# First products of two experts: over 336 and then 112 columns, or once over all 448, with idle products in the wait

## What is computed

```
x = x + tanh(g_xattn) * attention(layernorm(x), ctx, w_q, w_k, w_v, w_o)
h = layernorm(x)
expert e (16 of them, 2 shared and 14 routed):
    silu((h * rsqrt(mean(h*h) + eps) * rms_w[e]) @ W1[e]) @ W2[e]      # 128 -> 256 -> 128
gates = softmax(h @ router_w), the two largest kept and scaled to sum 1
x = x + tanh(g_ffn) * (sum of shared experts + gated sum of routed experts)
```

## Time and profile before

| what | us |
|---|---|
| median of 3 runs | 121.24 |
| lowest and highest run | 121.11 and 122.18 |
| the profiled execution's own time | 121.09 |
| its span, first to last instruction | 119.3 |
| PE busy in it | 109.5 |
| DVE busy | 69.1 |
| ACT busy | 59.3 |
| POOL busy | 43.8 |

### The profile page before, as it was taken

The page is one execution under the profiler, slowest core; times in us unless marked ns, Lnnn a source line. Parts: engine busy times, 40 slices in busy tenths (PEclk is TensorE's granted clock), DMA queues, the critical chain, the costliest instruction groups (busy, mean ns, idle before and its releaser), DMA issues.

```text
span 119.3 us, 2340 instructions
## 1 busy us (share of the span) xinstructions
PE 109.5 (92%) x800; PEld 93.7 (79%) x800; DVE 69.1 (58%) x195; ACT 59.3 (50%) x99; POOL 43.8 (37%) x75
## 2 busy tenths in 40 slices
PE   6976999994999999999789989999999999999980
PEld 6965978763458559459569989999999999999980
DVE  0069857775749859959921626998633333333361
ACT  4072983439379578678674279423333323333300
POOL 7703599000000100100100578666666666664000
PEclk9999999997699999999999999999999999999999
DMA  3999999999991000000000000000000000000002
GB/s 104 334 273 370 413 419 408 417 434 438 426 410 63 3 0 0 0 0 5 0 0 5 0 0 5 3 0 3 0 0 5 0 0 0 0 0 0 0 0 77
DMA packets 3169, 13.76 MB, mean 115 GB/s; under 512 B 431, under 2 KB 1007, under 8 KB 2775
## 3 DMA queue, kind: packets, MB, share of 16 engines
q1 hardware_dynamic: 3159, 13.63, 29.9%
HBM read 13.40 MB, written 0.23 MB: 114 GB/s over the span
## 4 chain that ended last, share of the span: by engine, by line
PE 71%; DVE 17%; DMA 5%; ACT 3%; issue 1%; SPq 1%; DVEq 0%
PE score_ps L703 15%; PE attn_ps L703 7%; PE score_ps L514 7%; PE ring L696 6%; PE ring L697 5%; PE ring L698 5%; PE ring L557 5%; DMA ctx_headT<-in_ctx_headT_dram 5%; DVE probs L1007 4%; DVE row_sum L1000 3%; PE attn_ps L576 3%; PE ring L488 3%; PE ring L598 3%; PE ring L490 2%; PE ring L489 2%; PE score_ps L509 2%
## 5 line engine op out<-in xcount | busy, mean ns | idle before, releaser
L898 ACT ACTIVATE mixT<-ring 128x896 f32<-128x896 f32 x16 | 14.6, 917 | 27.0 <-PE ring L698 26.9
L703 PE MATMUL score_ps<-w,mixT 128*112 (+1 forms) x160 | 19.2, 273 | 0.2 <-ACT mixT L898 0.2
L703 PEld LDWEIGHTS score_ps<-w,mixT 128*112 128x112 f32 x160 | 18.7, 177 | 0.7 <-issue 0.3
L427 POOL TENSOR_TENSOR h_scale<-h_base,minus_half 112x1 f32<-112x1 f32 x4 | 2.2, 546 | 44.2 <-DVE h_base L1030 44.2
L1174 DVE SCALAR_TENSOR_TENSOR xn_rows<-score_ps,gates,xn_rows 112x128 f32<-112x128 f32 x36 | 10.1, 345 | 11.5 <-PE score_ps L703 11.3
L576 PEld LDWEIGHTS attn_ps<-wkq_space,mixT 128*112 128x112 f32 x128 | 14.2, 177 | 2.5 <-issue 2.5
L576 PE MATMUL attn_ps<-wkq_space,mixT 128*112 128x128 f32 x128 | 15.0, 275 | 0.2 <-ACT mixT L775 0.2
L696 PE MATMUL ring<-hT_hi,w_hi 128*128 128x448 f32 (+2 forms) x36 | 13.9, 387 | 0.1
L392 POOL TENSOR_TENSOR w_full<-w,columns 128x256 f32 (+1 forms) x16 | 9.8, 613 | 11.5 <-PE ring L698 10.5
L697 PE MATMUL ring<-hT_lo,w_hi 128*128 128x448 f32 (+2 forms) x36 | 12.6, 350 | 0.0
L698 PE MATMUL ring<-hT_hi,w_lo 128*128 128x448 f32 (+2 forms) x36 | 12.6, 349 | 0.0
(11 more groups left out here) (133 smaller groups left out, 190.2 us busy)
## 6 DMA issues: line engine op xcount, KB each, us to landing
ctx_all<-in_ctx_dram SPq DMA_DIRECT2D x4, 1500.0 KB, 17.7
w<-in_w_dram SPq DMA_DIRECT2D x2, 1792.0 KB, 25.9
wkq_space<-in_wkq_dram SPq DMA_DIRECT2D x2, 512.0 KB, 4.5
wvo<-in_wvo_dram SPq DMA_DIRECT2D x1, 1024.0 KB, 9.1
w<-in_w_shared_dram SPq DMA_DIRECT2D x2, 256.0 KB, 15.2
ctx_head<-in_ctx_head_dram SPq DMA_DIRECT2D x1, 480.0 KB, 7.2
ctx_headT<-in_ctx_headT_dram SPq DMA_DIRECT2D x1, 224.0 KB, 5.6
x_space<-in_x_rows_dram SPq DMA_DIRECT2D x1, 224.0 KB, 6.2
```

The costliest lines, as they stand in the source:

```text
L703: last = nc.tensor.matmul(dst, hidden[slot][:, c, t * ROWS:(t + 1) * ROWS], w2_chunk(c), start=(c == 0), stop=(c == 1))
L898: nc.scalar.activation(hidden[slot], ring[:, 2 * slot:2 * slot + 2, 0:TOKENS], ACT.Silu).then_inc(S["hidden_ready"], 1)
```

## The change

Where the PE list had the products of experts 0 and 1 over the first 336 columns, sixteen idle products now stand, and the first group of logits follows them. After the last tile's columns are ready, both experts are made over all 448 columns. The waits on `w1_scaled_ready` move with the products. `hidden_filled` is raised by the same calls as before.

```diff
+ROW_PRODUCTS = 16
...
             pe.wait_ge(S["hT_ready"], 1)
-            for e in range(2):
-                pe.wait_ge(S["w1_scaled_ready"], e + 1)
-                hidden_products(e, h_parts[0][1])
+            keep_warm(ROW_PRODUCTS, score_ps[:, 0, 0:P])
             pe.wait_ge(S["columns_loaded"], 16)
             router_logits(0)
...
             keep_warm(SPLIT_PRODUCTS, score_ps[:, 0, 0:P])
             pe.wait_ge(S["hT_ready"], 2)
-            hidden_products(0, h_parts[1][1]).then_inc(S["hidden_filled"], 1)
+            pe.wait_ge(S["w1_scaled_ready"], 1)
+            hidden_products(0).then_inc(S["hidden_filled"], 1)
             router_logits(1).then_inc(S["logits_filled"], 1)
-            hidden_products(1, h_parts[1][1]).then_inc(S["hidden_filled"], 1)
+            pe.wait_ge(S["w1_scaled_ready"], 2)
+            hidden_products(1).then_inc(S["hidden_filled"], 1)
             pe.wait_ge(S["w2_shared_loaded"], 16)
             pe.wait_ge(S["hidden_ready"], 1)
             expert_output(0, 0, static_w2(0))
```

## The result

The changed kernel took 121.77 us (median of 20 runs, 121.26 to 123.43), the kernel before 121.05 us in the same comparison (median of 20, 120.50 to 122.82). The ratio is 1.0064 with a 95% interval of 1.0038 to 1.0091: 0.8 us slower, by 0.5 to 1.1. The profiled execution took 121.70 us with a span of 119.9, against 121.09 and 119.3.

A forecast was written before the change was run, and what follows sets the result against it. PE was taken to bound the kernel to its end, with the last tile's turning held by DVE and POOL. Terms -0.07 + 0.73 - 0.07 gave +0.6 us on the 121.24 median, 121.85 us, range 121.2 to 122.6.

The forecast's parts named there:

- What bounds the wait: Before the last tile's turning: DVE's rows, held by POOL, set the end at 67.61, not PE's 1.84 us of products.
- The estimate for that point, 1.7 us of products: In the wait for the last tile: idle products cost nothing while they take up to 1.7 us.
- The gain of 0.07 at the turning: At the last tile's turning: PE starts at 67.65, not 67.72, 0.04 after the rows; bounds 0 and 0.11.
- The sign that I had named: In the changed profile: the turning's weight load comes 2.44 us after the end of the attention's loads.
- Wide products in the open: Behind the last tile: first product to first output product takes 2.71 us against 1.98, a loss of 0.73.
- What closes up: Expert 0's output to the next group: 1.66 us, not 1.73, as PE comes without a wait; gain 0.07.
- What could be late next: POOL, ACT and DVE work for later experts moves later but keeps its cover, the thinnest some 0.3 us (the exponential).
- The chain view: Rival, wait for the last tile: the 1.84 us of products held the turning, so 1.2 us faster, 120.0; chance 0.04.
- the late gates: Rival, later experts: exponential and DVE's gate chain slip past their cover and PE waits, 122.35 us; chance 0.05.
- The overlap of wide products: Rival, behind the last tile: wide products stand only 0.11 us apart, so no change, 121.3 us; chance 0.03.
- The falling clock: Rival, behind the thinly filled wait: PE's clock halves for 3.4 us, up to 1.7 us more, 123.5; chance 0.12.

The follow-up runs named there:

- e1: Changed kernel with the twelve 336-column products back in place of the sixteen idle ones, their sums unused; 121.95 us against 121.00, ratio 1.0106.
- e3: Changed kernel without the sixteen idle products in the wait, the ten behind the turning kept; 122.55 us, ratio 1.0117, 4 runs.
- e4: Changed kernel with 48 idle products in the wait instead of sixteen; 123.08 us, ratio 1.0182.
- e8: Changed kernel without the wait for the last residual in front of the wait for the last normalised rows; 122.79 us, one run.
- e11: e9 without the wait for the residual in front of the wait for the last rows; 119.76 us, ratio 0.9897.
- e9: Kernel before plus early SiLU of 336 columns, two early output tiles of expert 0, and expert 2's weights scaled early into third buffers; 119.78 us, ratio 0.9907.
- e2: Kernel before with expert 0 still in two parts, but expert 1 made once over 448 columns behind the last tile; 121.29 us, ratio 1.0038.
- e6: Changed kernel without the sixteen idle products, the same as e3 run again; 123.11 us, ratio 1.0157, 6 runs.
- e5: Changed kernel without the sixteen idle products and without the ten behind the turning; 123.30 us, ratio 1.0143.

## Why the prediction was right, point by point

*The number.* The forecast of 121.85 us lies 0.08 from the 121.77 measured, and part of that is luck. It added 0.6 to the median of three runs, 121.24, where twenty runs gave 121.05; the starting point was 0.19 too high and the effect, 0.72 between the medians, was forecast 0.12 too low. The effect is the better test of the working.

*What bounds the wait.* Right: the chain through DVE and POOL, not PE's products. e1 shows it with the products present, e3 with nothing there, and e4 shows where PE begins to count. The estimate for that point, 1.7 us of products, fits e4: 0.83 us late with 2.77 us of them leaves 1.9.

*The gain of 0.07 at the turning.* This term was mis-sized: it measured 0 (2.20 and 2.21). I had taken 0.04 us from the ready rows to PE, from another release. Here it is 0.11 in both kernels: rows at 67.61, load at 67.72 before; 67.52 and 67.63 after. So I had misread the kernel before: the end of the logit loads at 67.73 beside the turning's load at 67.72 didn't make PE's way the last. DVE's release was the last already, and nothing was left to uncover. The sign that I had named shows the same: the turning's load was to come 2.44 us behind the end of the attention's loads, and it came 2.52 behind (67.63 less 65.11), as it had 2.51 behind before. e8 shows what most of the 0.07 were: PE has two waits in front of this turning, and with one it is 0.06 less; e11 repeats it against e9, 2.15 and 2.22.

*Wide products in the open.* Right in mechanism, 0.77 and not 0.73. The first group to the second took 70.05 - 68.61 = 1.44 (forecast 1.45), by two small errors that cancel: the six products took 1.32 and the logits 0.12, where I had 1.28 and 0.17. And the second to the output 1.31 (forecast 1.26): its first product, of which I expected 0.03 more than of the others, stands 0.29 from the next as it does behind an output, though it stands behind logits here. This term is nearly the whole result, and e2 confirms its shape, where the SiLU of expert 0 hides most of one wide group.

*What closes up.* Right: 1.66 and not 1.73, 0.07.

The sum in the trace is 0.01 + 0.77 - 0.07 = 0.71 us against a forecast of 0.6. *What could be late next* kept its cover as computed: POOL ended at 72.23 (forecast 72.3, wanted at 73.0), the exponential at 74.03 (74.0) with DVE's chain at 74.35 (74.3), and the addition of expert 1 ended at 82.51, where PE's next output into that bank began at 83.22, 0.71 apart as before.

*The rivals.* The chain view fell with the result, which was slower and not 1.2 us faster, and with e1; the late gates did not come. The overlap of wide products fell with the rows: behind their first one they stand 0.20 to 0.21 apart here too, not the 131 ns that the Trainium skill gives for 512 columns in "TensorE: Matmul & The Clock Gate", section "Back-to-back issue gap". The falling clock did not decide the median of this kernel, but its price was real: 1.3 us in e6 and 1.6 in e5, where I had said up to 1.7. What I had not seen is that the sixteen idle products seem to be what keeps it rare (16 of 20 runs under 122.0 us against 2 of 10). Four of the changed kernel's twenty runs lay at 122.8 or more; whether a fall at this place made them is open, since none of them has a profile and e8 shows another place that costs 1.1.

## What to carry to other kernels

When the chain view runs through an engine that is busy, look at what the other engines do at its end before the work is counted as path: where two ways end within a tenth of a microsecond, the chain can name the one that does not hold, and taking work from it gives nothing. Work done ahead in a wait is worth what it takes off the way that ends last behind the wait, and not its own time: 1.84 us of products were worth 0.71, and those of expert 1 alone 0.14, because a SiLU covered the rest. Idle products in the same place shorten nothing; at best they guard the clock. The most is had by drawing the next steps in as well (e9: by the distances 1.26 us under the kernel before and 1.97 under the changed one). And each such gain has to be followed to the next buffer that an idle engine could have filled earlier.

## What the hardware showed that I had not expected

The granted clock falls at different places in different executions of the same or nearly the same kernel, and the price depends on the place. From 28 to 32 us it fell in the kernel before, in e3 and in e5, and the last residual starts there at 65.52, 65.42 and 65.36; where the clock stayed full up to there it starts at 65.42 (changed kernel), 65.01 (e1) and 65.49 (e4). PE has slack in that stretch: in the changed kernel it is busy 2.46 of the 4 us. At 11 us a fall cost 1.1 us against the changed kernel's profile (residual at 66.54 in e8, 66.50 in e6), at 69 us 1.3 to 1.6. In the profile of e8, stretches the granted clock being the figure behind the count in brackets:

```profile
10.00:12.00 2.00, 1.09 (x4) 0.80 1.02 424
12.00:14.00 2.00, 2.00 (x7) 0.50 0.99 406
```

The kernel before did the same from 10 to 12 us, 1.07 us busy behind a pause of 0.93 where e8 has 1.09 and 0.91, and kept the full clock; so the work ahead, as these rows give it, does not tell whether the clock falls. Equal mean clocks hide times that are 1 us apart (121.14 and 122.21 in two runs of the kernel before, both at 0.986). And taking away a wait that was met long ago, in front of one that is not, brought the turning's load forward by 0.06 and 0.07 us, in the two pairs of profiles that differ by it (e8, e11).
